# Feed-forward rows 0 to 5 turned by a transposing DMA, written in bfloat16 by ScalarE

## The reference

```python
def bit_linear(x, w, b):
    gamma_x = jnp.clip(jnp.max(jnp.abs(x), axis=-1, keepdims=True), 1e-05, None)
    scale_x = 127.0 / gamma_x
    x_dq = jnp.clip(jnp.round(x * scale_x), -128.0, 127.0) / scale_x
    ...
    return jnp.einsum('bsd,hd->bsh', x_ste, w_ste) + b
gate = jax.nn.silu(bit_linear(x, gate_w, gate_b))     # 512 -> 2048
val = bit_linear(x, val_w, val_b)                     # 512 -> 2048
return bit_linear(gate * val, out_w, out_b)           # 2048 -> 512
...
x = x + _L0_xattn_ref(_layernorm(x, axis=-1), ctx_512, ...)
x = x + _L0_ffn_ref(_layernorm(x, axis=-1), ...)
```

## Time and profile before

| | |
|---|---|
| median of 3 runs | 848.12 us |
| the profiled execution, its own time | 844.1 us |
| its span | 842.3 us |
| busy over the span: TensorE, VectorE | 751.9 us (89%), 761.8 us (90%) |
| ScalarE, GpSimd | 573.9 us (68%), 578.4 us (69%) |
| SyncE's queue of DMAs, share of 16 engines | 63.9%, nearly all of it in the heads |
| mean granted TensorE clock | 0.974 |

### The profile page before, as it was taken

The page is one execution under the profiler, slowest core; times in us unless marked ns, Lnnn a source line. Parts: engine busy times, 40 slices in busy tenths (PEclk is TensorE's granted clock), DMA queues, the critical chain, the costliest instruction groups (busy, mean ns, idle before and its releaser), DMA issues.

```text
span 842.3 us, 13224 instructions
## 1 busy us (share of the span) xinstructions
PE 751.9 (89%) x3268; PEld 480.8 (57%) x3268; DVE 761.8 (90%) x1026; ACT 573.9 (68%) x838; POOL 578.4 (69%) x581
## 2 busy tenths in 40 slices
PE   3678999999999999999999999999999686868996
PEld 2545666766666666666666666666666442424453
DVE  5899999999999999999999999999999767887896
ACT  2587677767776877687677777776777577774332
POOL 4769684968496758776776768586849475967462
PEclk9999999999999999999999999999999797979999
DMA  9226887785768486859676767677669999400001
GB/s 327 81 72 112 166 150 135 144 173 125 155 130 177 104 173 131 173 115 175 124 151 141 153 132 152 140 153 148 139 147 217 240 230 261 182 0 26 13 25 38
DMA packets 298503, 118.54 MB, mean 141 GB/s; under 512 B 275952, under 2 KB 282096, under 8 KB 298224
## 3 DMA queue, kind: packets, MB, share of 16 engines
q1 hardware_dynamic: 297664, 116.70, 63.9%
q10 hardware_dynamic: 816, 1.57, 0.5%
HBM read 49.02 MB, written 2.10 MB: 61 GB/s over the span
## 4 chain that ended last, share of the span: by engine, by line
DVE 39%; PE 32%; issue 16%; ACT 7%; POOL 3%; DMA 1%; DVEq 1%; SPq 0%; ACTq 0%; POOLq 0%
PE banks L1519 9%; DVE neg_max L1328 9%; DVE rows L1339 6%; PE scores L1760 5%; PE banks L1460 3%; PE scores L1547 3%; DVE acc L1323 3%; PE banks L1775 3%; DVE cv_lo L1293 2%; DVE rot_sin L1302 2%; DVE rest L1275 2%; DVE rot_cos L1300 2%; ACT rows L1201 2%; PE banks L1474 1%; PE banks L1492 1%
## 5 line engine op out<-in xcount | busy, mean ns | idle before, releaser
L1190 ACT ACTIVATE scores<-scores,neg_max 128x1024 f32<-128x1024 f32 x128 | 139.1, 1087 | 61.6 <-DVE neg_max L1328 61.1
L1519 PE MATMUL banks<-pt,v_hi 128*128 128x512 f16 x512 | 162.0, 383 | 11.8 <-DMA pt<-rows 7.5
L1339 DVE SCALAR_TENSOR_TENSOR rows<-scores,rows 128x1024 f16<-128x1024 f32 x128 | 154.6, 1218 | 16.4 <-ACT rows L1201 15.2
L1328 DVE TENSOR_REDUCE neg_max<-scores 128x1 f32<-128x1024 f32 x128 | 155.2, 1213 | 2.9 <-PE scores L1547 2.7
L1060 POOL TENSOR_TENSOR rot_cos<-rot_cos,rot_sin 128x512 f32<-128x512 f32 x93 | 119.1, 1281 | 42.6 <-DVE rot_sin L1302 37.7
L1201 ACT ACTIVATE rows<-scores 128x1024 f16<-128x1024 f32 x128 | 131.0, 1023 | 5.2
L1068 POOL TENSOR_TENSOR rot_lo<-rot_cos,rot_hi 128x512 fp32r<-128x512 f32 x93 | 119.9, 1290 | 7.7
L1519 PE MATMUL banks<-pt,v_lo 128*128 128x512 f16 x256 | 98.7, 386 | 0.0
L1323 DVE SCALAR_TENSOR_TENSOR acc<-banks,inv,acc 128x512 f32<-128x512 f32 x128 | 91.2, 743 | 6.1 <-PE banks L1529 2.2
L1519 PEld LDWEIGHTS banks<-pt,v_hi 128*128 128x128 f16 x512 | 49.3, 98 | 80.6 <-issue 31.7
L1164 ACT CAST cv_hi<-banks 128x512 fp32r<-128x512 f32 x64 | 37.5, 587 | 83.6 <-PE banks L1460 42.0
(11 more groups left out here) (213 smaller groups left out, 1788.5 us busy)
## 6 DMA issues: line engine op xcount, KB each, us to landing
load<-in_pack SPq DMA_DIRECT2D x15, 320.0 KB, 3.0
raw_chunk<-in_out_w SPq DMA_DIRECT2D x8, 512.0 KB, 5.1
raw_chunk<-in_gate_w SPq DMA_DIRECT2D x8, 512.0 KB, 4.6
raw_chunk<-in_val_w SPq DMA_DIRECT2D x8, 512.0 KB, 4.0
pt<-rows SPq DMA_TRANSPOSE x256, 3.3
raw<-in_gate_w SPq DMA_DIRECT2D x8, 512.0 KB, 5.4
raw<-in_val_w SPq DMA_DIRECT2D x8, 512.0 KB, 5.0
raw<-in_out_w SPq DMA_DIRECT2D x8, 512.0 KB, 7.2
```

Source lines behind the costliest of these rows:

```text
L1190: nc.scalar.activation(scores[:, u % 2, :], scores[:, u % 2, :], ACT.Exp, bias=neg_max[:, u:u + 1], accum_out=sums[:, u:u + 1]).then_inc(e ...
L1328: nc.vector.tensor_reduce(neg_max[:, u:u + 1], scores[:, u % 2, :], AX, ALU.max, negate=True).then_inc(max_ready, 1)
L1339: nc.vector.scalar_tensor_tensor(out=rows[:, u % ROWS, 1, :], in0=scores[:, u % 2, :], scalar=WEIGHT_LIFT, in1=rows[:, u % ROWS, 0, :], op ...
L1519: mm = nc.tensor.matmul(out, t[x][:, b * LC + c, :], pt[:, b, :, low * LC + c, :], start=n == 0, stop=n == 3 * LC - 1)
```

## The change

For rows 0 to 5 the turn on TensorE and the copy from PSUM are gone. VectorE clips the lifted row at both ends in place (`clip`, float32, where `round_down` stood); ScalarE takes the magic number off and writes h_quant in bfloat16 (`drop`, at the end of its tile); SyncE's queue turns all of it from SBUF to SBUF in one transposing DMA (`turn_row`), and `contract` waits for its landing. Rows 6 and 7 go on as before. `contract` and `finish` of row h-2 move from behind projection 4 to behind projection 6 of tile h (`CONTRACT_BEHIND`). The loop over rows 4 to 7 is written out, so that each row's waits are constants of its own: projection 0 of tile 4 waits for five tokens taken, not for eight. The heads are not touched.

```diff
+ROWS_BY_DMA = 6
+    CONTRACT_BEHIND = 6
     def run(engine, tile, after):
-        for n in range(U):
+        for n in range(NU):
             tile(Head(n), min(n, 2))
-        with engine.Fori(0, (NU - U) // 2) as i:
-            for odd in range(2):
-                tile(Head(U + odd, i), 2)
         after(Head(NU - 2), Head(NU - 1))
         def turn(h):
-            pe.wait_ge(h_rounded, h.after(1, 1))
+            pe.wait_ge(h_rounded, h.after(1, 1) - ROWS_BY_DMA)
         def contract(h):
-            pe.wait_ge(ht_ready, h.after(1, 1))
+            if h.number < ROWS_BY_DMA:
+                pe.wait_ge(h_landed, 16 * h.number + 16)
+            else:
+                pe.wait_ge(ht_ready, h.number - ROWS_BY_DMA + 1)
@@ TensorE's tile
-                if before == 2 and n == 1:
-                    turn(h.plus(-2))
-                if before == 2 and n == 4:
+                if before == 2 and n == CONTRACT_BEHIND:
                     contract(h.plus(-2))
@@ VectorE
+        def clip(h):
+            row = hidden[:, h.number % 2, :]
+            dve.wait_ge(h_lifted, h.after(1, 1))
+            nc.vector.tensor_scalar(row, row, MAGIC + 127, MAGIC - 128, ALU.min, ALU.max).then_inc(h_clipped, 1)
         def round_down(h):
             dve.wait_ge(h_lifted, h.after(1, 1))
+            dve.wait_ge(h_landed, 16 * ROWS_BY_DMA)
@@ VectorE's tile
-                if before == 2 and n == 1:
-                    copy_ht(h.plus(-2))
                 if before and n == (3 if before == 1 else 2):
                     range_of(h.plus(-1))
-                if before == 2 and n == 4:
+                if before and n == 6 and h.number <= ROWS_BY_DMA:
+                    clip(h.plus(-1))
+                elif before and n == 5 and h.number > ROWS_BY_DMA:
+                    round_down(h.plus(-1))
+                if before == 2 and n == CONTRACT_BEHIND:
                     finish(h.plus(-2))
-                if before and n == (6 if before == 1 else 5):
-                    round_down(h.plus(-1))
@@ ScalarE
+        def drop(h):
+            act.wait_ge(h_clipped, h.number + 1)
+            if h.number:
+                act.wait_ge(h_landed, 16 * h.number)
+            nc.scalar.activation(h_quant[:], hidden[:, h.number % 2, :], ACT.Identity,
+                                 bias=t["minus_magic"][:]).then_inc(h_dropped, 1)
@@ ScalarE's tile, behind its four silus
+            if before and h.number <= ROWS_BY_DMA:
+                drop(h.plus(-1))
@@ GpSimd's tile
                 if before == 2 and n == 0:
-                    pool.wait_ge(h_rounded, h.after(1, -1))
+                    pool.wait_ge(h_dropped, h.after(1, -1))
@@ SyncE's tile
             if before == 2:
                 store(h.plus(-2))
+            if before and h.number <= ROWS_BY_DMA:
+                turn_row(h.plus(-1))
+        def turn_row(h):
+            sp.wait_ge(h_dropped, h.number + 1)
+            if h.number:
+                sp.wait_ge(out_full, h.number)
+            sp.dma_start(ht[:], h_quant[:], transpose=True).then_inc(h_landed, 16)
```

More of the change, by code:

```diff
@@ L1719, in feed_forward @@
     last_turned, last_copied = sem("last_turned"), sem("last_copied")
+    h_clipped, h_dropped, h_landed = sem("h_clipped"), sem("h_dropped"), sem("h_landed")
     out_tiles = out.rearrange("b (u p) d -> (b u) p d", p=P)
@@ L1850, in copy_ht @@
         def copy_ht(h):
-            dve.wait_ge(ht_full, h.after(1, 1))
+            dve.wait_ge(ht_full, h.after(1, 1) - ROWS_BY_DMA)
             nc.vector.tensor_scalar(ht[:].rearrange("p c s -> p (c s)"), ps_h[:], -128.0, None,
@@ L1976, in tile @@
                 pool.wait_ge(out_bias_loaded, 16)
-            if h.i is not None:
+            if h.number >= U:
                 pool.wait_ge(second.normed_ready, NU)
```

## The result

| | before | after |
|---|---|---|
| median of 5 runs each, us | 848.12 | 841.73 (840.68 to 845.37) |
| ratio of times, 95% interval | | 0.9947 (0.9924 to 0.9969) |
| run again in another session | 0.9997 (0.9981 to 1.0014) | 0.9919 (0.9891 to 0.9948) |
| the profiled execution, own time and span | 844.1, 842.3 | 845.37, 843.6 |
| granted TensorE clock, mean | 0.974 | 0.962 |

What follows compares the result with a forecast made beforehand. TensorE was taken to bound the rows, VectorE just below. The terms 3.6 - 0.5 + 0.1 + 1.7 + 0.3 gave 5.2 us, less 0.5 for hand-overs 4.7: 848.1 to 843.4 us, range 841.0 to 848.2.

Steps and rivals of the forecast that it cites:

- TensorE, tiles 4 to 7: Turns of rows 2 to 5 leave TensorE, 3.6 us gained, less 0.5 of stalls over four rows.
- The first chain: Closed chain over two tiles, contraction through scales, clip, drop and DMA: 8.23 + T/2 a row, 10.48 us.
- T: Time from issue to landing of the DMA that turns a row: 4.5 us taken, bounds 3.2 and 5.8.
- the second chain: Closed chain through the single buffer ht, contraction, finish, store issue, DMA: 4.88 + T, no bound before T = 5.5.
- Rival B: The DMA's whole issue comes before any data flows, T = 5.8, gain 1.3, 846.8 us; 16%.
- Rival E: T near 3 to 4 and contraction 0 at full clock, no stalls, 841.4 us; 11%.
- Clip and drop: VectorE's clip taken at 1.22 us (bounds 1.22 and 2.16), ScalarE's drop at 1.99.
- Tiles 2 and 3: Contraction 0 starts 3.3 us later, at half clock; idle time and two turns gone pay for it: gain 0.1.
- Tile 4's head: Projection 0 needs five tokens, not eight; its 1.99 wait goes and the clock stays up: gain 1.7 us.
- The end: Last projection's scale follows at once with a copy less, 0.3 of 1.0 us counted; end chain behind it unchanged.
- C: The half clock moves into tile 3 instead of going: gain 2.1 us, 846.0; 14%.
- D: The DMA sets the pace; gains and losses cancel at T = 6.2, 851.0 us at T = 7; 12%.

Runs made afterwards that it cites:

- unroll_behind6: Kernel before with its loop written out and contraction and finish moved behind projection 6, turn still on TensorE, no DMA; 847.31 us, ratio 0.9996.
- dma_twice: Changed kernel with a second transposing DMA per row, into a buffer nobody reads, ahead of the real one; 855.62 us, ratio 1.0076.
- two_halves: Changed kernel with drop and DMA in two halves of 1024 columns, contraction waiting for the second only behind its eighth matmul; 840.70 us, ratio 0.9916.
- after again: The changed kernel, unaltered, run and profiled a second time in a later session; 841.68 us, ratio 0.9919 to the kernel before.
- before again: The kernel before, unaltered, run and profiled a second time; 848.27 us, ratio 0.9997.
- wait_for_eight: Changed kernel with projection 0 of tiles 4 to 7 again waiting for all eight tokens taken; 843.29 us, ratio 0.9942.
- unroll_only: Kernel before with its loop over rows 4 to 7 written out and each row's own waits, nothing else; 844.98 us, ratio 0.9970.
- dma_behind7: Changed kernel with contraction and finish one projection later, behind projection 7; 850.15 us, ratio 1.0019.
- drop_by_vector: Changed kernel with the drop on VectorE, directly behind its clip, in place of ScalarE; 850.23 us, ratio 1.0023.
- four_rows: Changed kernel, rows 0 and 1 turned by TensorE, contracted behind projection 4; tokens taken before tile 3's silus; 838.69 us, ratio 0.9887.
- takes first: Changed kernel with ScalarE taking tokens 4 to 7 ahead of tile 3's silus instead of behind them; 841.73 us, ratio 0.9913.

## Why the prediction was right, step by step

**TensorE, tiles 4 to 7 (3.6 less 0.5 of stalls, 3.1; measured 3.2).** From 778.41 to 820.67 it is 42.26 us for four rows; without the token turn of 0.43 that fell into the first, 10.46 a row, against 10.35 of work. That is 0.43 of stalls in all where 0.5 was summed, and 4 x (11.25 - 10.46) = 3.2 won. (The 3.4 against unroll_behind6 has 0.2 of the end in it.) The first chain gives 8.23 + 4.3 / 2 = 10.38 with the measured T; two rows took 10.37. dma_twice and two_halves moved T both ways and the pace followed: upwards along the second chain, downwards to the bare work.

**T.** 4.3 to 4.5 where 4.5 was taken. The data flows while the instruction is still being issued: the one of 760.24 holds the queue until 762.17, and by 761.6 the DMA engines are busy (their share is the last number but one):

```profile
761.20:761.60 0.40, 0.40 (x2) 0.14 (x1) 0.40 (x1) 0.40 (x1) 0.40 (x1) 0.50 0.37 72
761.60:762.00 0.40, 0.40 (x2) 0.15 (x1) 0.40 (x1) 0.04 (x1) 0.40 (x1) 0.50 1.12 216
```

Rival B is out. Rival E's T of 3 is out too; its other half, contraction 0 at full clock, came true. The rule of the Trainium skill (Advanced Engine Details and Errata, X-Bar Transpose) from which that T would follow, that on trn2 transposing DMAs are as fast as regular ones, isn't borne out here: 256 KB turned take 3.2 us to land in two_halves, and a plain store of 256 KB, to the output, 2.0; 512 KB turned take 4.3.

**Clip and drop (1.22 and 1.99; measured 1.22 and 2.00).** The choice of the nearer row over four times the smaller form was right, and the clip of row 0, beside GpSimd, took the 2.00 foretold.

**Tiles 2 and 3 (0.1; measured 2.7 by the two first profiles, 0.1 by the two later ones, 0.9 and 1.9 across).** Against the profile that it was worked from, this is the mis-sized term. The step that failed: "TensorE has then waited, so I charge half clock as before". Contraction 0 ran in 3.63 us, in both profiles of after; the low clock came ahead of it, over projections for which TensorE had time to spare (busy 10.84 of 15.45 us). In the first of them it also began 1.06 us earlier than worked out (764.57 less the 7.53 by which tile 2 is later, 757.04 instead of 758.1): the drop started 0.8 sooner than I had put it, the rest is T. Together 2.7, of which 2.6 shows (36.61 worked out from tile 2 to tile 4, 34.04 measured). In after again the drop starts 9.88 us after tile 2, where I had put 9.91, and the 0.8 is gone. The half clock in the profile of before was chance, as before again shows, so some 1.8 of the 2.7 belongs to no edit. That the two later profiles give the very 0.1 of the sum is luck: it charged a half clock on both sides, and neither of them has it. Of the token waits, the first was 1.29 as I had worked it out from the takes (some 1.5), and the second 0.43 (0.5).

**Tile 4's head (1.7; measured 1.7, 57.09 - 55.44 with the loop written out alone).** The size is right and the reason isn't. "Its projection 0 now needs five tokens, not eight, so the 1.99 wait isn't there to repeat" holds for the unrolling alone. In the changed kernel wait_for_eight shows that the contraction's new place does it without the new count; and in unroll_behind6, which has no DMA, token 7 is likewise taken (781.89) just when tile 4 begins (781.86).

**The end (0.3; measured 0.4).** From the start of tile 7's turn to the last contraction it is 834.98 - 824.99 = 9.99 us; before it was 835.41 - 825.0 = 10.4 from the same point, when the last projection is out. What spoils the profile of after is the half clock of the last contraction, 5.30 for 3.62. In after again it ran in 3.62, and the contraction of before did as well. Of the 0.4, some 0.2 comes with the contraction's place, since unroll_behind6 has 10.20 there. Over all profiles the last contraction ran slow, in 4.1 to 5.3 us, in eight of eleven, and in none of the three that have neither the DMA nor the contraction behind projection 6 (before, before again, unroll_only). Whether an edit makes it likelier isn't shown; it would take back up to 1.7 us, which the prediction put at nothing ("The end chain behind it, to 839.07, is unchanged").

**The sum.** From tile 4 to the last contraction the three terms make 1.7 + 3.2 + 0.4 = 5.3 us, and 57.09 - 51.82 is 5.3. The reserve of 0.5 for hand-overs wasn't needed. With it the prediction said 4.7; the comparisons say 4.5 (ratio), 6.4 (medians) and 6.9 (0.9919, the later session), with intervals of 2.6 to 6.4 and 4.4 to 9.2 for the two ratios. So the size is borne out and the 0.2 between 4.7 and 4.5 is luck. Rivals C and D are out for this kernel: the low clock didn't move into tile 3 (1.00 from 764.57 to 783.16), and the DMA doesn't set the pace. C's mechanism does show in dma_behind7 and drop_by_vector, where token turns waited 2.30 and 3.10 us in tile 3.

**By parts, in measured time:** the unrolling alone wins 2.5 us, moving the contraction gives nearly all of it back (847.31), and the DMA wins 4.2 to 6.5 from there (0.9996 to 0.9947, and to 0.9919); wait_for_eight, run beside unroll_behind6, is 4.0 us below it by the medians. The change as a whole is thus worth about what its DMA is: its other two parts nearly cancel.

**Open:** whether four_rows is truly faster than the change and why; whether its three ideas (takes first, two halves, four rows) add up wasn't tried.

## What to carry to other kernels

A DMA that replaces work of the bounding engine pays as long as every closed chain through it stays below that engine's work per pass: write each chain as a + T / passes, and look for the T at which it crosses. Here there were two, 8.23 + T / 2 and 4.88 + T, and 2.5 to 3.7 us more of T, where the second binds, turned a gain of 0.5 to 0.8% into a loss of 0.8%. Two places earlier for the consumer cost nearly 4%. Moving the consumer to make room has a price too, in what it used to cover. When the unchanged part of a program differs by more between two profiles than the change is worth, measure from anchors, and profile both kernels twice before a half clock is put down to an edit.

## What the runs showed of the hardware

- Where the low clock falls scatters from execution to execution of the same program: the same contraction, behind a gap of 2.18 and of 2.50 us, took 5.30 us (before, 0.50 granted) and 3.63 (before again). The heads, unchanged, took 6.6 us more in the profile of after than in that of before.
- A transposing DMA from SBUF to SBUF costs 3.2 us for 256 KB and 4.3 for 512 KB, so 1.1 us for the second half. Of two large ones back to back the first lands 4.3 to 4.6 us after its own issue, the second 4.8 to 5.7.
- In-place clipping of 128x2048 float32 on VectorE takes 1.22 us, as long as writing bfloat16; where it begins while a GpSimd product is under way such an instruction takes 1.73 to 2.17, and a product that begins under it takes 2.15 for 1.28.
